# One decoder layer on one core: second attention and experts joined into one program, the last batch routed inside the expert loop

## The chip, the core and the metric

The kernel runs on one core of a Trainium2 chip. The core has five engines with an instruction queue each: TensorE (PE, matmuls and transposes), VectorE (DVE), ScalarE (ACT), GpSimd (POOL), and SyncE (SP), which here only issues DMAs. An engine works through its queue in order, and a wait on a semaphore holds everything behind it on that queue. TensorE's clock is granted at one of two levels, 1.2 and 2.4 GHz; the profile gives it as a share of full speed. The metric is the device time of one execution in microseconds.

## The reference, cut to what matters

Eight batches of 512 tokens with 256 features pass through a pre-norm decoder layer with three parts, each added to its input:

```python
x = x + attn(layernorm(x))            # first attention, linear in the tokens
x = x + xattn(layernorm(x), ctx)      # second attention: 16 heads of 64, causal, keys and values from ctx
x = x + ffn(layernorm(x))             # 16 experts, 4 per token
# ffn, for hidden states h:
probs = softmax(h @ router_w + router_b)
topw, topi = top_k(probs, 4); topw = topw / topw.sum()
out = sum over experts e of (gelu(h @ w1[e] + b1[e]) @ w2[e] + b2[e]) * combine[:, e]
```

w1 is 16 x 256 x 512, w2 is 16 x 512 x 256, all in float32.

## The kernel before

Matmuls on float32 data are done in three passes: each operand is split into a high part (a copy rounded by ScalarE or VectorE to fp32r) and a low part (the difference, by VectorE or GpSimd), and `split3` multiplies low by high, high by low and high by high. So each weight costs splitting work before it can be used.

There are three programs in a row, each in a block of its own: `first_attention`, `cross_attention` and `experts`. At the end of a block all engines meet at a barrier.

**Second attention.** `attention_plan` writes out by hand the order of the steps, and every engine walks through the same list and does its part of each step. Work goes by pairs of heads: n = 0 to 63, eight pairs (p = 0 to 7) for each of eight batches. For a pair there are `scores`, `soften` (maximum and exp), `even` (division by the sum), `turn` (transposes of the probabilities), `weigh` (the product with v) and `keep` (the split of the result). Between them stand the steps of neighbours: projections, `output` of the batch before, its normalisation (`find3`, `norm3`), and its routing: `transpose_x3`, `route`, `choose`, `mark`, `weigh_gates`, `place`, `turn_gates`, `add_b2`. `scatter` steps send a batch's rows, each with its token number and gate weights, by GpSimd's indirect DMA into a table in DRAM (`expert_rows`), sorted by expert; there are 16 such DMAs for a batch.

After pair 63 only the last batch's tail is left: `output`, `find3`, `norm3` and the whole routing chain. The w2 weights of the 16 experts are loaded over the attention's weights by seven DMAs in pairs 4 to 7, and are split (`high_w2` on ScalarE, `low_w2` on VectorE) after pair 63. `tables` computes for the first 20 expert tiles which expert and which rows they have; these tiles are certain from the first seven batches. `first_loads` loads x and w1 of tiles 0 and 1.

**Experts.** A tile is 256 rows of one expert; there are 79 tiles. The loop of `experts` in round j does, for different tiles: `load_w1` j+4, `load_x` j+4 (both issued by SP), `transpose` j+1 (TensorE turns x; ScalarE makes the high part, VectorE copies token number and gates to `tail` and makes the low part), `hidden` j (24 matmuls with 256 columns, gelu and high part on ScalarE, low part on VectorE), `split_w1` j+2 (VectorE), `results` j-1 (24 matmuls, scaling by the gate on ScalarE, two indirect adding DMAs by GpSimd into `out`). The loads have NX = 5 buffers for x and NW = 3 for w1, so load_x(j) waits for the transpose of tile j-5 and load_w1(j) for the split of tile j-3. Three of the five x buffers are free only later: one belongs to `experts`, two lie in `xn3`, the last batch's rows, and so the loads of tiles 3 and 4 wait for the 16 scatters of the last batch, which stand first in GpSimd's queue.

Inside the loop the tables of the other tiles are computed (rounds 5 to 12), and `pad` stores two experts' padding rows a round (four DMAs by SP, rounds 6 to 13). From tile 20 on a load waits for these. The additions of a tile wait for those of the two tiles before it where these may touch the same tokens. Behind the last filled tile there are some empty ones, which always wait.

Of the kernel before, what the change touches and what calls it, by code (L numbers as in the profile page):

```python
# [30 lines left out]
FULL_AT_LEAST = -(-((B - 1) * S * TOPK - E * (ROWS - 1)) // ROWS)  # L31
SURE_TILES = 20
# [7 lines left out]
NY = 3  # L40
# [80 lines left out]
class Kept:  # L121


    def __init__(self, nc, stack, ahead):
        sb = lambda name, shape, dtype=F32: stack.enter_context(nc.sbuf_tensor(f"kept_{name}", shape, dtype))
        self.xn3 = sb("xn3", [P, N_TILES, PAY])
        self.rows_i = [sb(f"rows{i}", [P, N_TILES, TOPK], I32) for i in range(2)]
        self.x_in = [sb(f"x{i}", [P, RT, PAY]) for i in range(2)]
        self.used, self.warm = sb("used", [P, E]), sb("warm", [P, 1])
        self.b1T = ahead.bits[:].rearrange("p a b -> p (a b)").bitcast(F32)[:, 0:E * FC]  # L130
# [106 lines left out]
def f32(ap):  # L237
    return ap.bitcast(F32)
# [738 lines left out]
def cross_attention(nc, sems, spent, d, x1_dram, x1_stored, out, rows_dram, routing, W, projecting, ahead, kept, hold):  # L977

    with ExitStack() as stack:
        p = Phase(nc, stack, sems, "xa")  # L980
        sb, signal, landed = p.sb, p.counts, p.landed
        plan = attention_plan()
# [11 lines left out]
        norms = {n: tuple(sb(f"ln{n}_{part}", shape) for part, shape in  # L994
                          (("stats", [P, N_TILES, 6]), ("mv", [P, N_TILES, 2]), ("rstd", [P, N_TILES]))) for n in (2, 3)}
# [4 lines left out]
        sums = [sb(f"sums{i}", [P, N_TILES, 2]) for i in range(2)]  # L1000
        xn3 = kept.xn3
# [10 lines left out]

        heads = ExitStack()
        own = lambda name, shape, dtype=F32: heads.enter_context(nc.sbuf_tensor(f"xa_{name}", shape, dtype))
        v = [own(f"v{i}", [P, N_TILES, INNER // 2]) for i in range(2)]
        q = [[own(f"q{i}{part}", [P, S], F32R) for part in ("hi", "lo")] for i in range(2)]
        k = [[own(f"k{i}{part}", [P, S], F32R) for part in ("hi", "lo")] for i in range(2)]
# [42 lines left out]
        w2_in, w2_hi = [landed(f"w2_in{i}", [i]) for i in range(len(LOAD_W2))], signal("w2_hi", W2_ORDER)  # L1060
# [5 lines left out]
        first_in = landed("first_x0", [0]), landed("first_x1", [1]), landed("first_w0", [0]), landed("first_w1", [1])  # L1066
# [7 lines left out]
        freed_by = []  # L1074
        for step, at in plan:
# [4 lines left out]
            if by is not None:  # L1080
                bank_of[step, at] = turn
                freed_by.append(by)
                turn += 1

        def bank(step, at):
            return work[bank_of[step, at] % len(work)]

        def sync(sp):
            w = Waits(sp)
            for step, at in plan:  # L1090
                if step == "load":
                    b = at
                    w.wait_ge(x2_ev, (b - 2, 1, 1), b >= 2)
                    w.wait_ge(x1_stored[b % 2], b)
                    sp.dma_start(x1[b % 2][:], x1_dram[b]).then_inc(x1_in[b % 2].of(b), 16)
                    w.wait_ge(c_lo, b - 1, b >= 2)
                    sp.dma_start(ctx32[:], d['ctxT'][b].rearrange("(k p) s -> p k s", p=P)).then_inc(ctx_in.of(b), 16)
                elif step == "add_b2" and at[1] == 1:
                    b = at[0]
                    w.wait_ge(b2_ev, at)  # L1100
                    sp.dma_start(out[b * S:(b + 1) * S, :].rearrange("(t p) c -> p t c", p=P), x2[:]
                                 ).then_inc(x2_out.of(b), 16)
                elif step == "load_w2":
                    end, (first, last) = B * PAIRS - 1, LOAD_W2[at]
                    w.wait_ge(k_pe, end - PAIRS)
                    w.wait_ge(v_pe, v_tiles[-1])
                    w.wait_ge(k_pe, end, at >= 2)
                    w.wait_ge(s_pe, (end - 1, 1, 1), at >= 3)
                    w.wait_ge(q_pe, end, at >= 4)
                    w.wait_ge(s_pe, (end, (3, 2, 1)[at - 4], 1) if at >= 4 else None, at >= 4)  # L1110
                    sp.dma_start(f32(W2_lo[:, first * WE:last * WE]).rearrange("p (k n) -> p k n", n=D),
                                 d['w2'][first:last].rearrange("e (k p) n -> p (e k) n", p=P)).then_inc(w2_in[at].of(at), 16)
                elif step == "first_loads":
                    w.wait_ge(pos_pe, B - 2)
                    sp.dma_start(kept.b1T, d['b1T']).then_inc(b1_in.of(0), 16)
                    w.wait_ge(t_dve, ("landed", 2))
                    w.wait_ge(c_lo, B - 1)
                    w.wait_ge(x2_ev, (B - 2, 1, 1))
                    w.wait_ge(scattered[of_batch(B - 2)], (B - 2, *last_scatter))
                    for j, tile in enumerate((ahead.ctx32[:], ahead.x1_0[:].rearrange("p t c -> p (t c)").rearrange("p (k n) -> p k n", k=KC))):  # L1120
                        row = sp.value_load(routing["first_row"][0:1, j:j + 1], min_val=0, max_val=E * REGION - ROWS)
                        sp.dma_start(kept.x_in[j][:], rows_dram[bass.ds(row, ROWS), :].rearrange("(p a) c -> p a c", p=P)
                                     ).then_inc(first_in[j].of(j), 16)
                        own = sp.value_load(routing["owner"][0:1, j:j + 1], min_val=0, max_val=E - 1)
                        sp.dma_start(tile, d['w1'][bass.ds(own, 1)].rearrange("a (k p) n -> p (a k) n", p=P)
                                     ).then_inc(first_in[2 + j].of(j), 16)
            w.wait_ge(b1_in, 0)
            for i, load in enumerate(first_in):
                w.wait_ge(load, i % 2)

        def tensor(pe):
            w = Waits(pe)

            def work_bank(step, at):
                n = bank_of[step, at]
# [4 lines left out]
            for step, at in plan:  # L1140
                if step == "transpose_x":
                    b, c = at
                    w.wait_ge(ln[2]["norm"], b)
                    PJ = work_bank(step, at)
                    for t in range(N_TILES):
                        m = pe.transpose(PJ[:, t * P:(t + 1) * P], xn[:, t, c * P:(c + 1) * P], ident[:])
                    m.then_inc(x_pe.of(at), 1)
                elif step in ("project_k", "project_q"):
                    n = at
                    b, pr = divmod(n, PAIRS)  # L1150
                    if step == "project_k":
                        w.wait_ge(c_hi, b, b >= 1)
                        w.wait_ge(c_lo, b, b >= 1)
                        src, weights, projected = cT[b % 2], W["WkT"], k_pe
                    else:
                        w.wait_ge(x_hi, (b, KC - 1), b >= 1)
                        w.wait_ge(x_lo, (b, KC - 1), b >= 1)
# [765 lines left out]
```

## Time and profile before

| what | us |
|---|---|
| median of 3 runs | 1717.81 |
| lowest, highest | 1715.85, 1723.5 |
| the profiled execution, own time | 1717.56 |
| its span, first to last instruction | 1715.8 |
| TensorE busy | 1605.2 (94%) |
| VectorE, ScalarE, GpSimd busy | 1193.0, 1066.7, 507.0 |
| second attention, from about | 224 |
| border between second attention and experts | 1142 to 1226 |
| mean granted clock over the whole | 0.974 |

All times are counted from the span's first instruction. A row of a timeline gives start, length, engine, line, operation, written tile <- read tiles, and in brackets the idle time before it with what ended it. SPq, PEq and POOLq are the queues' own work: issuing DMAs, waiting. Busy times of TensorE contain what a lower clock adds.

### The profile page before, as it was taken

The numbers are of one execution on the slowest core, as the hardware profiler recorded it, in microseconds if no ns is written. First come the engines' busy times: TensorE is split into PE (matmuls) and PEld (weight loads), VectorE is DVE, ScalarE is ACT, GpSimd is POOL, SyncE is SP. The second block draws the span as 40 slices with busy tenths as digits, with TensorE's granted clock in tenths as the row PEclk, the third lists the DMA queues.
The fourth block names the chain that finished last, engine by engine and source line by source line (L and its number), as shares of the span: only waits on it lengthen the run. The fifth ranks groups of instructions, "written<-read, shape, count | busy, mean of one in ns | idle before, by whom it ended". The sixth has DMA issues, their size and how long they took to land. (4 is left out here: it accounts for less than half of the span.)

```text
span 1715.8 us, 35765 instructions
## 1 busy us (share of the span) xinstructions
PE 1605.2 (94%) x12470; PEld 1351.0 (79%) x12470; DVE 1193.0 (70%) x2754; ACT 1066.7 (62%) x2699; POOL 507.0 (30%) x430
## 2 busy tenths in 40 slices
PE   5899989999999999999999999985899999999995
PEld 4788866777777777776777777764899999999995
DVE  6888857667767677677766776677576666666662
ACT  4545547666766666666666666763566666666663
POOL 2434400000310301202103003033654546454544
PEclk9999989999999999999999999996999999999998
DMA  3121110000110100201101001063697777777773
GB/s 98 37 87 68 44 61 2 1 25 2 49 42 2 65 26 13 78 2 44 47 2 65 27 2 66 14 226 120 191 256 189 173 167 168 180 174 167 178 174 38
DMA packets 94976, 144.54 MB, mean 84 GB/s; under 512 B 12576, under 2 KB 55120, under 8 KB 94800
## 3 DMA queue, kind: packets, MB, share of 16 engines
q1 hardware_dynamic: 64176, 101.40, 18.6%
q0 software_dynamic: 28896, 38.62, 12.1%
q8 instruction: 103, 1.69, 0.4%
q10 hardware_dynamic: 1728, 2.23, 0.4%
q14 instruction: 73, 0.60, 0.1%
HBM read 90.76 MB, written 51.46 MB: 83 GB/s over the span
## 5 line engine op out<-in xcount | busy, mean ns | idle before, releaser
L1323 ACT ACTIVATE xa_prob<-xa_S,xa_nmax 128x512 f32<-128x512 f32 (+3 forms) x512 | 265.8, 534 | 127.2 <-DVE xa_nmax L1437 126.3
L1849 POOL DMA_INDIRECT out<-ex_y,ahead_bits x158 | 256.8, 1625 | 237.4 <-ACT ex_y L1778 117.7
L1730 PE MATMUL ex_H<-ex_xT,ex_w 128*128 128x256 f32 x1896 | 249.5, 288 | 2.1 <-DVE ex_xT L1815 2.1
L1744 PE MATMUL ex_Y<-experts_w_hi,ex_hT 128*128 x1264 | 239.5, 283 | 0.0
L1730 PEld LDWEIGHTS ex_H<-ex_xT,ex_w 128*128 128x128 f32 x1896 | 235.4, 194 | 2.7 <-issue 2.7
L1744 PEld LDWEIGHTS ex_Y<-experts_w_hi,ex_hT 128*128 128x128 f32 x1264 | 201.9, 191 | 0.0
L1437 DVE TENSOR_REDUCE xa_nmax<-xa_S 128x2 f32<-128x1024 f32 (+3 forms) x256 | 197.9, 815 | 1.2 <-PE xa_S L1196 1.2
L1600 POOL DMA_INDIRECT expert_rows<-kept_xn,kept_rows x112 | 110.8, 989 | 269.0 <-DVE xa_prob L1449 244.7
L1337 ACT ACTIVATE xa_probT<-xa_work 128x512 f32<-128x512 f32 x256 | 139.4, 601 | 79.1 <-PE xa_work L1208 79.1
L1821 DVE TENSOR_TENSOR ex_hT<-ex_h,ex_hT 128x512 fp32r<-128x512 f32 x158 | 109.0, 692 | 109.7 <-ACT ex_hT L1769 109.5
L1744 PE MATMUL ex_Y<-experts_w_lo,ex_hT 128*128 x632 | 178.4, 282 | 0.0
L1449 DVE TENSOR_SCALAR xa_prob<-xa_prob,xa_sums 128x512 f32<-128x512 f32 (+3 forms) x512 | 169.5, 385 | 6.8
L1778 ACT ACTIVATE ex_y<-ex_Y,ahead_bits 128x256 f32<-128x256 f32 x158 | 66.3, 471 | 160.9 <-PE ex_Y L1744 144.3
L1208 PE MATMUL xa_work<-ahead_ident,xa_prob 128*128 128x128 f32 x1280 | 158.9, 278 | 6.3 <-DVE xa_prob L1449 6.2
L1220 PE MATMUL xa_work<-xa_probT,xa_v 128*64 128x512 f32 (+3 forms) x1024 | 153.7, 443 | 0.7 <-ACT xa_probT L1334 0.7
L1208 PEld LDWEIGHTS xa_work<-ahead_ident,xa_prob 128*128 128x128 f32 x1280 | 139.8, 142 | 16.6 <-DVE xa_prob L1449 9.1
L1764 ACT ACTIVATE ex_h<-ex_H,ex_b 128x256 f32<-128x256 f32 x316 | 131.6, 470 | 9.5 <-PE ex_H L1730 8.7
L1444 DVE RECIPROCAL xa_sums<-xa_sums 128x2 f32<-128x2 f32 (+1 forms) x192 | 32.2, 168 | 144.4 <-ACT xa_prob L1323 144.4
L1220 PEld LDWEIGHTS xa_work<-xa_probT,xa_v 128*64 128x64 f32 x1024 | 68.4, 137 | 80.9 <-issue 67.1
L1744 PEld LDWEIGHTS ex_Y<-experts_w_lo,ex_hT 128*128 128x128 f32 x632 | 120.5, 191 | 0.0
L1323 ACT ACTIVATION_READ_ACCUMULATOR xa_prob<-xa_S,xa_nmax 128x1 f32 x512 | 108.4, 212 | 0.0
L1769 ACT ACTIVATE ex_hT<-ex_h 128x512 fp32r<-128x512 f32 x158 | 99.9, 633 | 5.1
(348 smaller groups left out, 3628.7 us busy)
## 6 DMA issues: line engine op xcount, KB each, us to landing
ahead_ctx<-in_w SPq DMA_DIRECT2D x27, 512.0 KB, 3.7
ahead_x<-in_w SPq DMA_DIRECT2D x26, 512.0 KB, 4.4
ahead_xn<-in_w SPq DMA_DIRECT2D x26, 512.0 KB, 4.0
kept_x<-expert_rows SPq DMA_DIRECT2D x32, 273.0 KB, 4.5
kept_xn<-expert_rows SPq DMA_DIRECT2D x31, 273.0 KB, 4.4
experts_w_lo<-in_w SPq DMA_DIRECT2D x5, 1024.0 KB, 6.0
ex_x<-expert_rows SPq DMA_DIRECT2D x16, 273.0 KB, 4.5
expert_rows<-ahead_spare SPq DMA_DIRECT2D x32, 136.5 KB
```

Source lines behind the costliest of these rows:

```text
L1208: m = pe.transpose(PJ[:, col:col + P], prob[n % 2][:, odd, PROB_AT[i] + j * P:PROB_AT[i] + (j + 1) * P], ident[:])
L1220: m = pe.matmul(OB[HD * odd:HD * odd + HD, j * P:512], v[n % 2][:, j, first_col + HD * odd:first_col + HD * odd + HD], probT[:, odd, PROB_ ...
L1323: m = act.activation(prob[n % 2][:, odd, PROB_AT[i]:PROB_AT[i] + width], SB[slot[at]][:, odd, col:col + width], ACT.Exp, bias=nmax[n % 2][ ...
L1337: act.activation(probT[:, odd, first_col:first_col + 512], bank(step, at)[:], ACT.Copy).then_inc(t_ev.of(at), 1)
L1437: m = dve.tensor_reduce(nmax[n % 2][:, i, :], SB[slot[at]][:, :, SCORE_COL[i]:SCORE_COL[i] + (i + 1) * P], AX.X, ALU.max, negate=True)
L1449: m = dve.tensor_scalar(part, part, sums[n % 2][:, i, odd:odd + 1], None, ALU.mult)
L1600: pool.indirect_dma_start(rows_dram, bass.IndirectOffsetOnAxis(rows_i[b % 2][:, t, k:k + 1], 0), xn3[:, t, :], None).then_inc(scattered[of ...
L1730: m = pe.matmul(bank[:, (f % 2) * ROWS:(f % 2 + 1) * ROWS], ww[:, c, f * P:(f + 1) * P], xx[:, c, :], start=(i == 0), stop=(i == len(terms ...
L1744: m = pe.matmul(bank[:, a * D:(a + 1) * D], hh[:, f, a * P:(a + 1) * P], W2[:, bass.ds(own * WE + f * D, D)], start=(i == 0), stop=(i == l ...
L1764: i = act.activation(h32[:, f, :], HB[2 * (j % 2) + u][:, (f % 2) * ROWS:(f % 2 + 1) * ROWS], ACT.Gelu, bias=b1[j % 2][:, f:f + 1])
L1821: dve.tensor_tensor(hT[j % 2][1][:, fs, :], h32[:, fs, :], f32(hT[j % 2][0][:, fs, :]), op=ALU.subtract).then_inc(h_lo.of((j, u)), 1)
L1849: pool.indirect_dma_start(out, bass.IndirectOffsetOnAxis(tail[j % NT][:, a, 0:1].bitcast(I32), 0), y[j % NY][:, a, :], None, compute_op=AL ...
```

## The change

- Second attention and experts become one block with one list of steps. The barrier between them goes; each expert step waits for the attention's semaphores that it needs (`gone`).
- The routing of the last batch (`CHAIN`) moves into rounds 1 to 10 of the expert loop, one piece a round, with a PSUM bank of its own (`ALONE`), and its 16 scatters into rounds 8 to 15, two a round. The expert tiles that come before must be certain without it: `tables` now runs after six batches and covers 24 tiles (`SURE_TILES`).
- w2 is loaded in another order and split in pieces: two pieces in pair 5, two in pair 6, three in pair 7, two beside the turns of pair 63, and seven around the last output projection. Two of the low parts (10 and 13) are made by GpSimd.
- The buffers that the two programs can't share any more are fewer: NX 5 to 2, NW 3 to 2. `load_x` is issued for tile j+2 in round j, `load_w1` for tile j+4 stands behind `split_w1` j+2. Tiles 0 to 11 are turned in one PSUM bank in place of two.
- The late tables move to rounds 8 to 14, the pads to rounds 9 to 16. The gelu table is loaded before round 0, and once more after the exp of the last batch's routing.
- The descriptor buffer of GpSimd's DMAs is set to 8192 bytes.

The diff, cut to its core (indentation that only follows from the new functions is left out):

```diff
-SURE_TILES = 20
+SURE_BATCHES = B - 2
+SURE_TILES = 24
...
-LOAD_W2 = ((2, 5), (5, 8), (12, 14), (14, 16), (8, 10), (10, 12), (0, 2))
+LOAD_W2 = ((2, 4), (4, 8), (14, 16), (0, 2), (12, 14), (8, 10), (10, 12))
-W2_ORDER, LOW_W2 = (3, 4, 5, 6, 7, 14, 15, 0, 1, 2, 8, 9, 10, 11, 12, 13), 13
+TURN_AT, LOW_BY_POOL = 14, (10, 13)
+CHAIN = {1: [("find3", B - 1)], 2: [("norm3", B - 1)], 3: [("transpose_x3", (B - 1, c)) for c in range(KC)], 4: [("route", B - 1)],
+         5: [("choose", B - 1)], 6: [("mark", B - 1), ("weigh_gates", B - 1)], 7: [("place", B - 1)], 8: [("turn_gates", B - 1)],
+         9: [("add_b2", (B - 1, 0))], 10: [("add_b2", (B - 1, 1))]}
...
         if n == B * PAIRS:
-            plan += [*turns, ("tables", None), *high_w2(0, 4), finish[0], *low_w2(0, 3), finish[1], *scatters]
+            plan += [*turns, *split_w2(6, 7), *finish, *scatters]
...
-            second += {4: [("load_w2", 0)], 5: [("load_w2", 1)], 6: [("load_w2", i) for i in (2, 3)],
-                       7: [("load_w2", i) for i in (4, 5, 6)]}.get(p, [])
+            second += {0: [("tables", 0)], 1: [("tables", 1)], 2: [("tables", 2), ("load_w2", 0)], 3: [("tables_turn", None)],
+                       5: [*split_w2(2, 3), ("load_w2", 1), *((step, j) for j in range(2) for step in ("load_x", "load_w1"))],
+                       6: [*split_w2(4, 5), *(("load_w2", i) for i in (2, 3))], 7: [*(("load_w2", i) for i in (4, 5, 6)), ("load_b1", None), *split_w2(14, 15)]}.get(p, [])
...
+             ("split_w1", 0), ("turn_x", 0), ("warm", None), *split_w2(8, 0), ("output", (b, 1, 0)),
+             ("output", (b, 1, 1)), ("load_w1", 2), ("split_w1", 1), *split_w2(10, 9, 13, 12, 11), ("load_w1", 3)]
+    for j in range(MOE_TILES + 1):
+        chain = CHAIN.get(j, [])
+        steps = [("load_x", j + 2), ("turn_x", j + 1), ("turn_tables", None), ("hidden", j), *chain[:1], ("split_w1", j + 2),
+                 ("load_w1", j + 4), ("results", j - 1), *chain[1:]]
...
+        plan += [("scatter_last", i) for i in (2 * (j - 8), 2 * (j - 8) + 1) if 0 <= i < ALL_ROWS]
+        plan += [("pad", e_) for e_ in (2 * (j - 9), 2 * (j - 9) + 1) if 0 <= e_ < E]
...
-NX, NW, NT, FIRST, TURN_AT = 5, 3, 5, 2, 12
+NX, NW = 2, 2
...
-            step_of = {"load_w1": j + 4, "load_x": j + 4, "transpose": j + 1, "hidden": j, "split_w1": j + 2, "results": j - 1}
...
                 elif step == "load_w1":
+                w.wait_ge(gone["t_dve"], ("landed", 2))
+                w.wait_ge(gone["c_lo"], B - 1)
+                w.wait_ge(gone["x2_ev"], (B - 2, 1, 1))
                     w.wait_ge(t_dve, ("landed", 2), j >= SURE_TILES)
                     w.wait_ge(w1_hi, j - NW, j >= NW)
...
                     bank = YB[j % 2]
                     w.wait_ge(y_ev, j - 2, j >= 2)
-                    w.wait_ge(low_w2, W2_ORDER[-1])
+                w.wait_ge(gone["low_w2"], 11)
+                w.wait_ge(gone["low_w2_pool"], 13)
...
-    nc = bacc.Bacc("TRN2", target_bir_lowering=False, num_devices=1)
+    nc = bacc.Bacc("TRN2", target_bir_lowering=False, num_devices=1, dynamic_dma_scratch_size=8192)
```

The new main loop, the same for every engine:

```python
plan = [*attention_plan(), ("finish", None)]
for step, at in plan:
    attend["sync"](sp, w, step, at)
    apply_experts["sync"](sp, w, step, at)
```

## Rows read from the trace of the kernel before

**Rows 1.** The page, part 1: busy time, share of the span, instructions.

```profile
PE 1605.2 (94%) x12470; PEld 1351.0 (79%) x12470; DVE 1193.0 (70%) x2754; ACT 1066.7 (62%) x2699; POOL 507.0 (30%) x430
```

**Rows 2.** Windows: stretch, length, busy us (instructions) by engine, clock, DMA share, GB/s.

```profile
1142.00:1226.00 84.00, 53.55 (x340) 46.72 (x341) 56.69 (x138) 40.70 (x71) 42.16 (x40) 0.74 0.49 157
...
1400.00:1690.00 290.00, 288.81 (x2431) 288.60 (x2430) 189.59 (x325) 190.03 (x420) 151.18 (x95) 1.00 0.72 167
```

**Rows 3.** The chain that ended last, 1183 to 1240: start, length, what.

```profile
1213.46 2.65 DMA expert_rows<-kept_xn,kept_rows
...
1216.85 3.19 DMA kept_xn<-expert_rows
...
1226.47 0.44 PE ex_X L1716 x4
...
1226.91 2.87 PE ex_H L1730 x24
...
1232.65 0.44 PE ex_X L1716 x4
```

**Rows 4.** Timeline of PE around the border: start, length, work [idle before].

```profile
1150.40 2.37 PE L1220 MATMUL xa_work<-xa_probT,xa_v 128*64 128x512 f32 x16 [0.74 <-ACT xa_probT L1334]
...
1155.65 0.36 PE L1237 MATMUL xa_work<-xa_Wo_hi,xa_oT_lo 128*128 128x256 f32 x1 [2.44 <-DVE xa_oT_lo L1464]
...
1191.24 1.09 PE L1716 MATMUL ex_X<-ahead_ident,kept_x 128*128 128x128 f32 x4 [8.31 <-PEq L1605]
```

**Rows 5.** Timeline of ACT and of DVE between 1154 and 1166.

```profile
1154.59 7.69 ACT L1367 ACTIVATE experts_w_hi<-experts_w_lo 128x1024 fp32r<-128x1024 f32 x8
...
1156.01 3.49 DVE L1534 TENSOR_TENSOR experts_w_lo<-experts_w_lo,experts_w_hi 128x1024 fp32r<-128x1024 f32 x3
...
1163.95 1.41 DVE L1382 BATCH_NORM_STATS2 xa_ln_stats<-xa_x 128x6 f32<-128x256 f32 x4
```

**Rows 6.** Groups of POOL's instructions by form: count, busy us, mean ns.

```profile
L873 POOL TENSOR_TENSOR WqT_lo<-ahead_ctx,WqT_hi 128x1024 fp32r<-128x1024 f32 x2 | 4.8, 2412 | 0.0
```

**Rows 7.** Timeline of all engines over two tiles.

```profile
1303.18 0.60 PE L1716 MATMUL ex_X<-ahead_ident,ex_x 128*128 128x128 f32 x4
...
1305.31 0.84 ACT L1764 ACTIVATE ex_h<-ex_H,ex_b 128x256 f32<-128x256 f32 x2
...
1309.57 1.23 DVE L1804 TENSOR_TENSOR ex_w<-ahead_ctx,ex_w 128x1024 fp32r<-128x1024 f32 x1
...
1311.60 0.39 SPq L1699 DMA_DIRECT2D ahead_ctx<-in_w  x1
...
1312.82 0.34 SPq L1685 DMA_DIRECT2D kept_x<-expert_rows  x1
...
1315.54 0.60 PE L1716 MATMUL ex_X<-ahead_ident,kept_xn 128*128 128x128 f32 x4
```

**Rows 8.** Waits of SP's queue, 1290 to 1660: total us, times, longest.

```profile
SPq L75 <- DVE ex_w L1804: 222.8, 59, 6.1
```

**Rows 9.** DMA issues, three windows of the expert loop: count, KB, median us to landing.

```profile
kept_xn<-expert_rows SPq DMA_DIRECT2D x23, 273.0 KB, 4.5
...
kept_xn<-expert_rows SPq DMA_DIRECT2D x1, 273.0 KB, 3.0
...
kept_xn<-expert_rows SPq DMA_DIRECT2D x1, 273.0 KB, 6.0
```

**Rows 10.** Timeline of SP's queue with the pad stores.

```profile
1243.60 2.79 SPq L1692 DMA_DIRECT2D expert_rows<-ahead_spare  x4
...
1247.21 0.41 SPq L1699 DMA_DIRECT2D ahead_xn<-in_w  x1
```

**Rows 11.** Timeline of PE, the last hidden step.

```profile
1687.69 3.02 PE L1730 MATMUL ex_H<-ex_xT,ex_w 128*128 128x256 f32 x24
```

**Rows 12.** The chain that ended last, its end.

```profile
1701.18 3.77 DMA out<-ex_y,ahead_bits
...
1707.68 1.55 POOL out L1849
```

More of the change, by code:

```diff
@@ L1059, in cross_attention @@
         id_set = signal("id_set", batches)
[L1060 removed]
+        w2_in, w2_hi = [landed(f"w2_in{i}", [i]) for i in range(len(LOAD_W2))], signal("w2_hi", [at for step, at in plan if step == "high_w2"])
+        low_w2, low_w2_pool = (signal(n, [at for step, at in plan if step == "low_w2" and (at in LOW_BY_POOL) == mine])
+                               for n, mine in (("low_w2", False), ("low_w2_pool", True)))
         x3_pe, x3_ev = signal("x3_pe", blocks), signal("x3_ev", blocks)
@@ L1079, in cross_attention @@
                   "tables_turn": (t_dve, ("landed", 2))}.get(step)
-            if by is not None:
+            if (step, at) in ALONE:
+                alone_after[step, at], last_alone = last_alone, by
+            elif by is not None:
                 bank_of[step, at] = turn
@@ L1085, in bank @@
         def bank(step, at):
+            if (step, at) in alone_after:
+                return SB[0][:, 1, :]
             return work[bank_of[step, at] % len(work)]
[L1088 to L1129, printed above, removed]
@@ L1138, in work_bank @@
                 return work[n % len(work)]
[L1140 to L1157, printed above, removed]
-                        src, weights, projected = xT, W["WqT"], q_pe
-                    PJ = work_bank(step, at)
-                    for c in range(KC):
-                        for i, (ww, xx) in enumerate(split3(weights, src)):
-                            m = pe.matmul(PJ[:], ww[:, c, pr * P:(pr + 1) * P], xx[:, c, :],
-                                          start=(c == 0 and i == 0), stop=(c == KC - 1 and i == 2))
-                    m.then_inc(projected.of(n), 1)
-                elif step == "project_v":
-                    n, t = at
-                    b, half = divmod(n, 2)
@@ new lines, in tensor @@
+            if step == "transpose_x":
+                b, c = at
+                w.wait_ge(ln[2]["norm"], b)
+                PJ = work_bank(step, at)
+                for t in range(N_TILES):
+                    m = pe.transpose(PJ[:, t * P:(t + 1) * P], xn[:, t, c * P:(c + 1) * P], ident[:])
+                m.then_inc(x_pe.of(at), 1)
+            elif step in ("project_k", "project_q"):
+                n = at
+                b, pr = divmod(n, PAIRS)
+                if step == "project_k":
@@ L1605, in cross_attention @@
-        with nc.Block() as block:
-            block.tensor(tensor)
-            block.scalar(scalar)
-            block.vector(vector)
-            block.gpsimd(gpsimd)
-            block.sync(sync)
-        return x2_out, scattered
-NX, NW, NT, FIRST, TURN_AT = 5, 3, 5, 2, 12
-def experts(nc, sems, d, rows_dram, out, routing, held, ahead, kept, x2_out, sent):
+            elif step == "tables_turn":
+                w.wait_ge(tables_pe, 0)
+                tables.give_out(dve, t_dve, 0, bank(step, at), ahead, routing)
@@ L1619, in experts @@
+NX, NW = 2, 2
+CHAIN_END = 12
+LATE_ROOM = 2584
+def experts(nc, sems, d, rows_dram, out, routing, held, ahead, kept, gone):
     with ExitStack() as stack:
@@ L1657, in experts @@
         w1_hi, w1_lo, b1_ev = (signal(n, tiles) for n in ("w1_hi", "w1_lo", "b1_ev"))
-        w1_loaded = [landed(f"w1_loaded{i}", [j for j in tiles[i::NW] if j >= FIRST]) for i in range(NW)]
+        w1_loaded = [landed(f"w1_loaded{i}", tiles[i::NW]) for i in range(NW)]
         h_pe, gelu, h_hi, h_lo = (signal(n, halves) for n in ("h_pe", "gelu", "h_hi", "h_lo"))
         y_pe, y_ev = signal("y_pe", tiles), signal("y_ev", tiles)
-        plan = [("load_x", 2), ("load_w1", 2), ("split_w1", 0), ("transpose", 0), ("split_w1", 1), ("load_w1", 3), ("load_x", 3)]
```

1349 lines of the change are left out of this document (717 added, 632 removed).

## Prediction

> **What bounds the kernel now.** I read the page first. TensorE is busy for 1605.2 of 1715.8 us [rows 1], so time can come only from its idle stretches or from a slower clock. The windows place them: 84 us around the border between attention and experts hold 53.55 us of TensorE work at a mean granted clock of 0.74, while 290 us of the expert loop are 288.81 us busy at 1.00 [rows 2]. The chain around the border shows the loop's rhythm. The steps called X start at 1226.47 and 1232.65, so a tile takes 6.18 us, all of it matmuls (0.44 + 2.87 + 2.87), and the first tiles before that hang on the last scatters and on the loads behind them [rows 3]. TensorE's timeline gives the border's two ends: the last weighing of values starts at 1150.40, the output projection at 1155.65, the first expert transpose only at 1191.24 [rows 4].
>
> Names: t(j) is the time at which TensorE starts turn_x(j+1), the first step of round j. Before, t(4) = 1226.47 (rounds 0 to 3 turn tiles 1 to 4; x of tile 4 was the load that landed at 1220.04, and X of tile 5 starts at 1226.47).
>
> **Removed at the border.** The barrier, the routing of the last batch in an empty TensorE, and 16 scatters that stand ahead of tiles 3 and 4. TensorE's work there is not removed. The clock comes back with it.
>
> **The border after.** Rows 4 fix the start: output projection from 1155.65, since it waits for the last low part of the attention output, and VectorE reaches that as early as before. W2's splitting costs ScalarE 0.98 us a piece (7.69/8) and VectorE 1.16 us (3.49/3) [rows 5]. Seven pieces move into pairs 5 to 7 of the last batch, where TensorE sets the pace: taken as free there (if the cover is gone, 7 x 1.16 = 8 us). Two pieces go to GpSimd at 2.41 us each [rows 6], behind the 16 scatters that end near 1164; they are done near 1169, before round 1's results ask for them. The two projections are 48 matmuls like those of a tile half (2.87 us per 24), so t(0) = 1155.65 + 5.8 = 1161.5. VectorE then has, behind the attention output (ready 1155.1): 0.7 for b2, 2.1 for splitting w1 of tile 0, 0.9 for x, two pieces 2.3, two output additions that end near 1162.5, and w1 of tile 1, ready at 1164.6.
>
> **The part that decides: NX 5 to 2 and NW 3 to 2.** I followed one tile through all queues. From X at 1303.18, ScalarE's gelu starts at 1305.31, VectorE ends the low half of w1 at 1309.57 + 1.23 = 1310.8, SP issues the next w1 load at 1311.60 and the next x load 1.22 later, at 1312.82. TensorE is at the next-but-one X at 1315.54 [rows 7]. That is w1 issue = t(j) + 8.4, x issue = t(j) + 9.6. Before, these loads are for tiles far ahead. SP waits on this same split 59 times in 360 us [rows 8], and nobody is hurt.
>
> After, load_w1(j+4) waits for the split of w1(j+2), which VectorE makes in round j. load_x(j+3) stands behind it in SP's queue, although its own buffer has long been free. And x(j+3) is what TensorE needs first in round j+2. So
>
> t(j+2) = t(j) + 9.6 + landing of x.
>
> The landing is 4.5 us in the median of 23 loads; the shortest that I found took 3.0, one of the longest 6.0 [rows 9]. At 6.18 us a round only 12.36 - 9.6 = 2.7 us are to be had. None of the landings is so short. The period becomes (9.6 + 4.5)/2 = 7.05 us, 0.87 more, and TensorE is idle for 0.87 us in each round. At 6.18 of 7.05 us busy I leave the clock at 1.00. The splitting can't come earlier: it stands behind the tile's hidden step on VectorE, which follows matmul, gelu and copy.
>
> A page speaks to this term. The Trainium skill (DMA: Bandwidth & Descriptors, Anatomy of one DMA) fits one software-queued transfer as 2.0 us plus its bytes over 436 GB/s. For 273 KB that would be an estimate of 2.6 us, which lands in time, and the sum would be that of the first rival below. The trace disagrees: 4.5 us with the w1 load just ahead on the same queue, and 3.19 us with no load just ahead [rows 3].
>
> **First rounds.** x(2) is behind load_w1(3), which waits for 1164.6: t(1) = 1164.6 + 0.9 + 1.2 + 4.5 = 1171.2. VectorE has three more W2 pieces (3.5 us) before x(1), and ends w1(2) at 1172.1: t(2) = 1172.1 + 6.6 = 1178.7. Statistics for the last batch (batch norm 1.41 us [rows 5], about 2.0 with what follows) stand ahead of w1(3): t(3) = 1171.2 + 14.1 + 2.1 = 1187.4. Normalising (1.4) lies partly in slack: t(4) = 1194.3. That is 32.2 us earlier than 1226.47.
>
> **Rounds 4 to 78.** 75 rounds x 0.87 = +65.3 us. Routing steps ahead of a split in rounds 4 to 9 (0.7 to 2.2 us each: logits, exp with two table loads on ScalarE, marking, placing), each counting half, less what the even and odd chains absorb: +1.7. Tables in rounds 8 to 14: +2. The 32 pad stores: SP issues four in 2.79 us, and the next load starts 3.6 us after the first pad [rows 10]. After, they stand between load_w1(j+4) and load_x(j+3) in rounds 9 to 16, so x is issued 3.8 us later and lands behind their bytes, I take 0.5 more: 4.3/2 x 8 = +17. Before, rounds 4 to 78 held 3.4 us beyond 75 x 6.18, mostly waits for tables and for late additions, which a slower loop hides: -3.4. Sum: +82.6.
>
> The 16 scatters now fill GpSimd in rounds 8 to 15, two each, in the time that its additions leave. A smaller descriptor buffer for GpSimd's DMAs: at most two additions are issued per tile, so I take nothing; were each of 158 additions late by 0.3 us, they would still be within a round.
>
> **The end.** The last hidden step starts at 1687.69 [rows 11]; with it and two result steps TensorE ends at 1696.3, 19.5 us before the span's end. The last seven tiles wait for each other's additions, 6.6 us a link (4 us from issue to landing, and the last issue ends at 1709.2) [rows 12]. With 7.05 us a round GpSimd keeps up, and the end is 1.7 (scaling) + 1.8 (waiting for tile 77) + 3.4 (two issues) + 6.6 (as before) = 13.5 us behind TensorE: -6.
>
> **Sum.** 1715.8 - 32.2 + 82.6 - 6 = 1760.2 us of span. The profiled execution's own time was 1717.56, 1.8 above its span, and is within 0.3 us of the median of the runs (1717.81). So 1762 us. A measurement of this kernel can tell about 0.5% (8.6 us) from no change.
>
> **Rivals.**
> 1. The x loads land in time and the loop stays at 6.18 us: it would need landings below 2.7 us. Then VectorE's splits alone hold the first rounds: t(1) = 1169.0, when x(1)'s low part is ready, and three rounds of some 6.6 us follow, so t(4) is near 1189, 37.5 us earlier, the end is as before, and the time is 1680. For it: before, both loads travel among GpSimd's additions, and a slower loop could thin that traffic. Against: even the shortest landing is 3.0. Chance 0.12.
> 2. The landings shorten to 3.0 to 3.6 us. At 3.3 the period is 6.46: -35 at the border, 75 x 0.28 = +21, pads and the rest +14, so no change, 1718; at 3.0 it is 1705, at 3.6 about 1730. Chance 0.08, half of it within 0.5%.
> 3. Idle TensorE loses its clock. It did so at the border (0.74 [rows 2]). In the eight pad rounds of 9.2 us it is idle for 3. At half the clock there the first half of hidden is 1.4 us longer and results more: +10 to +30, so 1772 to 1795. Chance 0.15.
> 4. TensorE is slowed in pairs 5 to 7 by the moved splits by up to 8 us, with the rest as forecast: 1770. It is in the forecast's range.
>
> **Chances.** The forecast (landings of 3.6 to 5 us, 1730 to 1785) has 0.65. Landings of 5.0 us would give 7.3 us a round and 1784; that bounds it above. The range takes in rivals 2 and 4 and most of 3: 1703 to 1790, with 0.12 left out below and some 0.06 above. Faster by over 0.5%: 0.12 + 0.03 = 0.15. Within 0.5%: 0.05. Slower: 0.80.
>
> **What would show it.** Right: in rounds 20 to 70 X starts every 7.0 to 7.1 us; TensorE's idle time there, 60 us in all, is ended by the DMA of expert rows; SP's x load goes out 1.2 us behind the w1 load; t(4) near 1194 and no gap of more than 5 us at the border; rounds 9 to 16 the slowest. Wrong: X every 6.18 us in spite of landings over 2.7 us (then the order of SP's queue is not what binds), or a border that still has tens of idle microseconds, or a low clock in the loop.

## The result and the profile after

The changed kernel takes 1799.93 us in the median of four runs (1795.01 to 1804.69); the kernel before takes 1716.96 us beside it. The ratio is 1.0475, 95% interval 1.0436 to 1.0514. The forecast was 1762 with a range of 1703 to 1790. The sign and the mechanism held; the loss is 83 us where 45 were forecast, and the range ends below it. The profiled execution has a span of 1793.3 us where the sum gave 1760.2, so 33 us are to be found. It is the fastest of the four; the other 5 us to the median are in no trace and stay unexplained.

The page of the changed kernel, lines of its parts 1, 5 and 6 (the ones that answer to [rows 1] and [rows 9]):

```profile
PE 1623.1 (91%) x12470; PEld 1360.6 (76%) x12470; DVE 1195.2 (67%) x2752; ACT 1078.5 (60%) x2702; POOL 505.0 (28%) x432
...
L1732 PE MATMUL ex_X<-ahead_ident,kept_x 128*128 128x128 f32 x316 | 53.1, 293 | 89.4 <-DMA kept_x<-expert_rows 81.1
...
kept_x<-expert_rows SPq DMA_DIRECT2D x79, 273.0 KB, 4.5
```

TensorE has the same 12470 matmuls and is idle for 170 us, before for 111. Of the 170 us, 81.1 are ended by one thing, the landing of an x load in front of the turn of x (the steps called X). Its median landing is the 4.5 us of before [rows 9].

Windows of the changed kernel: the border, rounds up to 4, rounds 4 to 10, the pad rounds 10 to 18, rounds 18 to 77, and one single round in the last line (columns as in [rows 2]):

```profile
1140.00:1166.00 26.00, 20.00 (x140) 14.64 (x141) 20.39 (x34) 21.47 (x41) 15.97 (x15) 0.87 0.61 197
1166.00:1204.40 38.40, 27.22 (x195) 26.64 (x194) 28.94 (x48) 17.88 (x36) 15.97 (x9) 0.82 0.42 119
1204.40:1250.60 46.20, 40.46 (x351) 39.80 (x350) 29.71 (x87) 28.93 (x60) 20.70 (x18) 1.00 0.60 140
1250.60:1333.10 82.50, 60.85 (x424) 59.94 (x423) 37.40 (x81) 34.02 (x72) 40.76 (x31) 0.83 0.73 192
1333.10:1762.40 429.30, 378.52 (x3070) 370.29 (x3069) 242.34 (x414) 248.10 (x531) 186.43 (x118) 0.98 0.63 147
1356.10:1363.80 7.70, 7.70 (x53) 7.70 (x53) 2.64 (x5) 3.54 (x7) 3.09 (x2) 0.78 0.63 139
```

Before, the loop was busy 288.81 of 290 us [rows 2]. Now 59 rounds (t(18) to t(77)) take 429.3 us, 7.28 each, with TensorE busy for 378.52. The pad rounds take 82.5/8 = 10.3 us.

What one waits for, in rounds 18 to 77 (line waited for, us in total, times, longest), TensorE's and then SP's own:

```profile
PE ex_X L1732 <- DMA kept_x<-expert_rows: 50.6, 37, 2.2
...
SPq L76 <- DVE ex_w L1821: 287.3, 58, 7.7
```

SP stands on the split of w1 once a round, as before [rows 8], where it hurt nobody. Two rounds on the timeline (start, length), to lay beside [rows 7]:

```profile
1371.83 0.65 PE L1732 MATMUL ex_X<-ahead_ident,kept_x 128*128 128x128 f32 x4 [1.74 <-DMA kept_x<-expert_rows]
...
1378.03 0.60 PE L1732 MATMUL ex_X<-ahead_ident,kept_x 128*128 128x128 f32 x4
1378.28 1.23 DVE L1821 TENSOR_TENSOR ex_w<-ahead_x,ex_w 128x1024 fp32r<-128x1024 f32 x1
...
1380.29 0.38 SPq L1714 DMA_DIRECT2D ahead_x<-in_w  x1
1381.50 0.33 SPq L1697 DMA_DIRECT2D kept_x<-expert_rows  x1
...
1386.05 0.66 PE L1732 MATMUL ex_X<-ahead_ident,kept_x 128*128 128x128 f32 x4 [1.72 <-DMA kept_x<-expert_rows]
```

The split ends at 1379.51, the w1 load goes out at 1380.29 (t + 8.46), the x load 1.21 us behind it, and the next-but-one X starts 4.55 us after that. The two chains, of even and of odd tiles, are not evenly spaced: in many stretches rounds of 6.20 and of about 8.2 us take turns, and what counts is the sum of two (median 14.43 us in rounds 18 to 77).

### The profile page after: what moved, and what is told of

It reads as the page before. It is cut to its first block, busy times and chain, and to the rows that moved or that the text cites. A ratio compares the mean times of both kernels' runs of the same rounds, so it can differ in the third digit from the quotient of the medians.

```text
span 1793.3 us, 35763 instructions
## 1 busy us (share of the span) xinstructions
PE 1623.1 (91%) x12470; PEld 1360.6 (76%) x12470; DVE 1195.2 (67%) x2752; ACT 1078.5 (60%) x2702; POOL 505.0 (28%) x432
## 3 DMA queue, kind: packets, MB, share of 16 engines
q0 software_dynamic: 28896, 38.62, 11.4%
## 4 chain that ended last, share of the span: by engine, by line
PE 38%; ACT 18%; DVE 13%; DMA 10%; issue 5%; SPq 3%; POOL 0%; POOLq 0%; DVEq 0%; ACTq 0%
DMA kept_x<-expert_rows 9%; PE ex_H L1750 7%; ACT xa_prob L1334 7%; PE xa_work L1174 5%; PE xa_work L1249 5%; PE xa_S L1203 4%; PE xa_work L1185 4%; PE xa_work L1232 4%; PE xa_work L1220 4%; ACT xa_probT L1348 3%; DVE xa_nmax L1452 3%; DVE ex_w L1821 2%; ACT ex_h L1785 2%; PE ex_X L1732 2%; DVE xa_prob L1464 2%
## 5 line engine op out<-in xcount | busy, mean ns | idle before, releaser
L1867 POOL DMA_INDIRECT out<-ex_y,ahead_bits x158 | 249.6, 1580 | 327.4 <-ACT ex_y L1798 193.2
L1750 PE MATMUL ex_H<-ex_xT,ex_w 128*128 128x256 f32 x1896 | 265.8, 300 | 0.0
L1750 PEld LDWEIGHTS ex_H<-ex_xT,ex_w 128*128 128x128 f32 x1896 | 251.7, 207 | 0.0
L1785 ACT ACTIVATE ex_h<-ex_H,kept_b 128x256 f32<-128x256 f32 x316 | 131.7, 468 | 58.5 <-PE ex_H L1750 50.8
L1732 PE MATMUL ex_X<-ahead_ident,kept_x 128*128 128x128 f32 x316 | 53.1, 293 | 89.4 <-DMA kept_x<-expert_rows 81.1
L1732 PEld LDWEIGHTS ex_X<-ahead_ident,kept_x 128*128 128x128 f32 x316 | 36.0, 146 | 99.6 <-DMA kept_x<-expert_rows 91.3
```

The source lines that it names most:

```text
L1732: m = pe.transpose(x_bank(j)[:, c * ROWS + a * P:c * ROWS + (a + 1) * P], x_in[j % NX][:, a, c * P:(c + 1) * P], ident[:])
L1750: m = pe.matmul(bank[:, (f % 2) * ROWS:(f % 2 + 1) * ROWS], ww[:, c, f * P:(f + 1) * P], xx[:, c, :], start=(i == 0), stop=(i == len(terms ...
L1785: i = act.activation(h32[:, f, :], HB[2 * (j % 2) + u][:, (f % 2) * ROWS:(f % 2 + 1) * ROWS], ACT.Gelu, bias=b1[j % 2][:, f:f + 1])
L1867: pool.indirect_dma_start(out, bass.IndirectOffsetOnAxis(tail[j % NT][:, a, 0:1].bitcast(I32), 0), y[j % NY][:, a, :], None, compute_op=AL ...
```

## The experiments

Theory A, going into them: x arrives late because its load stands in SP's queue behind a w1 load that waits for VectorE; what counts is the time from its issue to the round that needs it, and a smaller number of buffers matters only through that. Theory B: two buffers for each of x and w1 are themselves too few at this load on the DMA queues, or the rest of the joined program costs the time. All ratios are against the kernel before, run beside it, with 95% intervals.

**1. The x load one tile further ahead.** The step that issued x of tile j+2 ahead of the turn now issues x of tile j+3 behind it, still with two buffers:

```diff
-        steps = [("load_x", j + 2), ("turn_x", j + 1), ("turn_tables", None), ("hidden", j),
+        steps = [("turn_x", j + 1), ("load_x", j + 3), ("turn_tables", None), ("hidden", j),
...
-             ("output", (b, 1, 1)), ("load_w1", 2),
+             ("output", (b, 1, 1)), ("load_x", 2), ("load_w1", 2),
```

> The changed kernel with one order changed: in round j SP issues the x load of tile j+3 right behind the transpose of tile j+1, ahead of the w1 load that waits for VectorE's split. Buffers (two for x, two for w1), traffic and all other work stay. Theory A (the x load is late only because it stands behind that w1 load in SP's queue): X starts every 6.2 us in rounds 20 to 70, TensorE's idle time ended by the DMA of expert rows (81 us) all but goes, the clock stays at 1.00 there, and the time is 1690 us, between 1680 and 1705. Theory B (two x buffers are too few, or the DMA engines are too busy, whatever the order): rounds stay at 7.0 us or more and the time above 1780 us.

Measured: 1694.23 us (1692.85 to 1695.74), 0.9847 [0.9823, 0.9871]. Two windows of this kernel, rounds up to 4 and 347 us of the loop:

```profile
1166.00:1204.40 38.40, 30.34 (x236) 30.17 (x235) 30.96 (x53) 20.79 (x44) 15.79 (x8) 0.87 0.49 142
...
1333.00:1680.00 347.00, 341.13 (x2888) 340.71 (x2886) 222.74 (x381) 226.09 (x498) 181.99 (x113) 1.00 0.72 166
```

Its timeline, SP's loads and TensorE's X:

```profile
1372.97 0.38 SPq L1714 DMA_DIRECT2D ahead_x<-in_w  x1
1374.18 0.33 SPq L1697 DMA_DIRECT2D kept_x<-expert_rows  x1
...
1376.70 0.60 PE L1732 MATMUL ex_X<-ahead_ident,kept_x 128*128 128x128 f32 x4
...
1382.83 0.60 PE L1732 MATMUL ex_X<-ahead_ident,kept_x 128*128 128x128 f32 x4
```

The x load still goes out 1.21 us behind the w1 load, and still takes 4.4 us in the median. But it now carries the tile of X at 1382.83 instead of 1376.70, so it has 8.65 us in place of 2.52. X follows every 6.13 us, TensorE no longer waits for x in the loop, and the clock is 1.00. A move of one step in SP's queue takes off some 106 us, more than the change had lost; theory A holds for this loss.

**2. The two buffers alone, in the kernel before.** NX = NW = 2 and the order of loads of the changed kernel; the barrier and the routing of the last batch stay as before. (One thing follows from the buffers: the x loads of tiles 3 and 4 no longer wait for the last batch's scatters.)

```diff
-NX, NW, NT, FIRST, TURN_AT = 5, 3, 5, 2, 12
+NX, NW, NT, FIRST, TURN_AT = 2, 2, 5, 2, 12
...
-            step_of = {"load_w1": j + 4, "load_x": j + 4, "transpose": j + 1, "hidden": j, "split_w1": j + 2, "results": j - 1}
+            step_of = {"load_x": j + 2, "transpose": j + 1, "hidden": j, "split_w1": j + 2, "load_w1": j + 4, "results": j - 1}
```

> The kernel before with one part of the change alone: NX = 2 and NW = 2 in the expert loop, load_x for tile j+2 at the head of round j, load_w1 for tile j+4 behind split_w1 j+2. Barrier, routing of the last batch, tables and pads stay where they were (the first x loads no longer wait for the last batch's scatters, since their buffers are free). Theory A: rounds of 7.3 us, rounds with pads of 10.3 us, so 67 x 1.1 + 8 x 4.1 = +107 us, less some 8 at the start and 6 at the end: about 1807 us. Theory B (the loss comes from the last batch's routing and scatters inside the loop, or from the joined program): 1717 us or less.

Measured: 1819.31 us (1818.79 to 1826.34), 1.059 [1.0558, 1.0622]. The loop, window of this kernel:

```profile
1420.00:1660.00 240.00, 211.61 (x1691) 207.57 (x1690) 134.47 (x229) 135.35 (x292) 101.58 (x64) 0.96 0.63 144
```

So buffers and order alone, without the joined program, cost 101 us, and by the two ratios (1.059 and 1.0475) the joined program gives some 20 back.

**3. Pads behind the next x load.** In the changed kernel, the four pad stores of a round are issued after the x load that follows them:

```diff
+        pads_of = lambda i: [("pad", e_) for e_ in (2 * (i - 9), 2 * (i - 9) + 1) if 0 <= e_ < E]
+        steps[1:1] = pads_of(j - 1)
...
-        plan += [("pad", e_) for e_ in (2 * (j - 9), 2 * (j - 9) + 1) if 0 <= e_ < E]
```

> The changed kernel with the pad stores of a round moved behind the next x load in SP's queue, so that they fill the time in which SP waits for the split. Theory A: rounds 9 to 16 fall from 10.3 us to some 7.5, in all -22 us, so 1778 us. If the pads cost by their traffic on the DMA engines and not by their place in the queue, the rounds stay near 10 us and the time near 1800.

Measured: 1783.29 us (1781.04 to 1785.29), 1.0366 [1.034, 1.0393]. Rounds 10 to 18 fall from 10.3 to 7.70 us, 21 us in all; the mean granted clock there is 0.97 in place of 0.83, so a part of the 21 is clock. t(10) is 3.3 us later than in the changed kernel, and rounds 18 to 77 came out at 7.39 instead of 7.28, which takes some back.

**4. Both late low parts by VectorE.** GpSimd splits none of w2:

```diff
-TURN_AT, LOW_BY_POOL = 14, (10, 13)
+TURN_AT, LOW_BY_POOL = 14, ()
```

> The changed kernel with the low parts of w2 pieces 10 and 13 made by VectorE in place of GpSimd. If GpSimd's additions hold VectorE up (three pieces took 5.6 us there and a 4-column copy 2.3 us while GpSimd worked on its two), five pieces take 5.8 us, and X of round 1 starts some 2 us earlier than 1177.5, in spite of more work. If VectorE is merely busy, X of round 1 starts 2.3 us later. In the time of the whole (1800 us) either is hardly to be seen.

One run: 1798.59 us, which can't be told from the changed kernel; the border's trace can. First the changed kernel's timeline at the border, with the last weighing of values (which began at 1150.40 before [rows 4]):

```profile
1156.10 2.38 PE L1232 MATMUL xa_work<-xa_probT,xa_v 128*64 128x512 f32 x16 [0.79 <-ACT xa_probT L1345]
...
1162.73 0.17 DVE L1826 COPY kept_b<-ahead_bits 128x4 f32 x1 [0.22 <-issue]
...
1166.02 0.60 PE L1732 MATMUL ex_X<-ahead_ident,kept_x 128*128 128x128 f32 x4
...
1168.49 5.98 POOL L1604 TENSOR_TENSOR experts_w_lo<-experts_w_lo,experts_w_hi 128x1024 fp32r<-128x1024 f32 x2
1168.82 2.33 DVE L1826 COPY kept_b<-ahead_bits 128x4 f32 x1
1171.06 5.62 DVE L1549 TENSOR_TENSOR experts_w_lo<-experts_w_lo,experts_w_hi 128x1024 fp32r<-128x1024 f32 x3
...
1176.70 0.68 DVE L1832 TENSOR_TENSOR ex_xT<-ex_X,ex_xT 128x512 fp32r<-128x512 f32 x1
...
1177.52 1.09 PE L1732 MATMUL ex_X<-ahead_ident,kept_x 128*128 128x128 f32 x4 [8.03 <-DVE ex_xT L1832]
```

And the same place with GpSimd out of it:

```profile
1164.03 0.60 PE L1732 MATMUL ex_X<-ahead_ident,kept_x 128*128 128x128 f32 x4
1166.83 0.17 DVE L1825 COPY kept_b<-ahead_bits 128x4 f32 x1
1166.90 5.76 DVE L1549 TENSOR_TENSOR experts_w_lo<-experts_w_lo,experts_w_hi 128x1024 fp32r<-128x1024 f32 x5
1173.49 1.08 PE L1732 MATMUL ex_X<-ahead_ident,kept_x 128*128 128x128 f32 x4 [6.00 <-DVE ex_xT L1831]
```

VectorE does all five pieces in 5.76 us, 1.15 each, where three took 5.62 beside GpSimd; a copy of 4 columns takes 0.17 in place of 2.33. From t(0) to t(1) it is 9.46 us in place of 11.50.

**5. Three orders together.** Experiments 1 and 4, and the pads between the x and the w1 load of the next round:

```diff
+        steps[2:2] = pads_of(j - 1)
```

> The changed kernel with three edits together: the x load ahead of the w1 load (1694 us alone), all low parts of w2 by VectorE (2.1 us at the border), and the pad stores of a round between the x load and the w1 load, where SP waits for the split anyway. With the x load first, rounds 13 to 16 still take 9.3, 7.6, 8.9 and 7.7 us, 8.9 us too much. If these are the w1 loads, late behind the pads in SP's queue, they go: 1694 - 2 - 8 = 1684 us. If they come from the pads' traffic on the DMA engines (busy to 1.00 there), they stay: 1692.

Measured: 1690.45 us (1687.09 to 1692.27), 0.9842 [0.9821, 0.9863]. The pad rounds fall to 6.5 us (7.3 in experiment 1) and t(1) to 1173.1 (1176.3). In the two traces that puts experiment 5 ahead by 8.5 us at t(77). The ratios to the kernel before, 0.9847 for experiment 1 and 0.9842 here, each with an interval of some 4 us to either side, don't show it: what pads and GpSimd's share are worth once x has 8.65 us of room stays between nothing and a few microseconds.

**6. x ahead of the w1 load, but behind the same wait.** Here the x load gets no more tiles of lead. It is issued at the moment when the w1 load may go, and in front of it:

```diff
-        steps = [("load_x", j + 2), ("turn_x", j + 1), ("turn_tables", None), ("hidden", j), *chain[:1], ("split_w1", j + 2),
-                 ("load_w1", j + 4), ("results", j - 1), *chain[1:]]
+        steps = [("turn_x", j + 1), ("turn_tables", None), ("hidden", j), *chain[:1], ("split_w1", j + 2),
+                 ("load_x", j + 3), ("load_w1", j + 4), ("results", j - 1), *chain[1:]]
...
+                w.wait_ge(w1_lo, j - 1, j >= 3)
```

> The changed kernel with the x load still behind the wait for the split of w1(j+2), but issued before the w1 load in place of after it. This tests the sum t(j+2) = t(j) + 8.5 (wait for the split) + 1.2 (issue of the w1 load) + landing. If the landing is long because 512 KB of w1 are ahead of it, it falls to some 3.2 to 3.5 us: 8.5 + 3.4 = 11.9, under two free rounds of 12.36, the rounds are near 6.3 us and the time is 1700 to 1715 us. If the landing keeps its 4.5 us whatever stands ahead, two rounds take 13.0, a round 6.5, and the time is 1740 us. If only the order behind the wait decides and no margin counts, it stays at 1785 or more.

Measured: 1705.47 us (1703.93 to 1707.1), 0.9934 [0.9911, 0.9957]. Page part 6 of this kernel, and its timeline with SP's two loads:

```profile
kept_x<-expert_rows SPq DMA_DIRECT2D x79, 273.0 KB, 2.8
```

```profile
1376.53 0.60 PE L1733 MATMUL ex_X<-ahead_ident,kept_x 128*128 128x128 f32 x4
1376.99 1.23 DVE L1822 TENSOR_TENSOR ex_w<-ahead_x,ex_w 128x1024 fp32r<-128x1024 f32 x1
1379.01 0.33 SPq L1698 DMA_DIRECT2D kept_x<-expert_rows  x1
1380.10 0.38 SPq L1715 DMA_DIRECT2D ahead_x<-in_w  x1
...
1382.66 0.60 PE L1733 MATMUL ex_X<-ahead_ident,kept_x 128*128 128x128 f32 x4
```

The X before these starts at 1370.4; the x load leaves 8.6 us behind it and is for the X at 1382.66. It lands in 2.8 us with the w1 load behind it, where it took 4.5 with that load ahead. 8.6 + 2.8 = 11.4 is less than two rounds of 6.13, and X follows every 6.14 us. The w1 load takes 5.0 in place of 3.7, which it can afford. This is the forecast's formula at its edge: 9.7 + 4.5 binds, 8.6 + 2.8 does not, with the same two buffers and the same wait. The kernel is still 11 us slower than that of experiment 1. In the traces the difference of span, 8.4 us, is spread over all stages: 1.5 us at t(4), 3.8 up to t(18), and 3.3 in rounds 18 to 77, where one round took 9.32.

**7. Two buffers in the kernel before, with x one tile further ahead.** Experiment 2 with the order of experiment 1:

```diff
-            step_of = {"load_x": j + 2, "transpose": j + 1, "hidden": j, "split_w1": j + 2, "load_w1": j + 4, "results": j - 1}
+            step_of = {"transpose": j + 1, "load_x": j + 3, "hidden": j, "split_w1": j + 2, "load_w1": j + 4, "results": j - 1}
```

> The kernel before with NX = 2 and NW = 2 (1819 us when the x load stood behind the w1 load) and the x load of tile j+3 right behind the transpose of tile j+1. Theory A: two buffers of each are enough when the order is right, the rounds are 6.2 us again, and the first tiles no longer wait for the 16 scatters: 1705 to 1717 us. If two buffers cost by themselves: above 1740 us.

Measured over ten runs: 1714.34 us (1708.06 to 1719.61), 0.998 [0.9965, 0.9996]. Its loop:

```profile
1420.00:1660.00 240.00, 240.00 (x2030) 240.00 (x2029) 159.77 (x274) 159.52 (x353) 127.70 (x80) 1.00 0.75 176
```

When each load is issued for the right tile, two buffers in place of five and three cost nothing in these 240 us and nothing in the whole, and theory B falls as the cause of the loss. The whole is a balance, though. In this trace t(4) is 9.4 us earlier than before, since tiles 3 and 4 no longer wait for the scatters; rounds 4 to 10 give back 3.7 of this, rounds 18 to 77 4.7 (two neighbouring rounds took 7.76 and 12.19 us in this execution), and the end 0.9. Whether the small losses belong to the buffers is open. Beside it, experiment 5 shows what the joined program, its pads moved too, is worth with the loads in order: 1714.34 - 1690.45 = 23.9 us.

**8. The seven moved splits of w2 put back.** Experiment 5 with w2's pieces 2 to 5, 14, 15 and 1 split behind pair 63 (pairs 6, 7 and 63 are cut in the same way as pair 5 here):

```diff
-                       5: [*split_w2(2, 3), ("load_w2", 1), *((step, j) for j in range(2) for step in ("load_x", "load_w1"))],
+                       5: [("load_w2", 1), *((step, j) for j in range(2) for step in ("load_x", "load_w1"))],
...
-             ("split_w1", 0), ("turn_x", 0), ("warm", None), *split_w2(8, 0), ("output", (b, 1, 0)),
+             ("split_w1", 0), ("turn_x", 0), ("warm", None), *split_w2(2, 3, 4, 5, 14, 15, 1, 8, 0), ("output", (b, 1, 0)),
```

> As the one with three edits, but the seven w2 pieces of pairs 5 to 7 are split behind pair 63 again. Prices the moved splits. In the changed kernel the last weighing ends 5.7 us later than before. If the moved splits are the reason, it ends some 4 to 6 us earlier here, but VectorE has 7 x 1.16 = 8.1 us more ahead of the first tiles, so the whole is 2 to 4 us slower than with three edits: 1687 us. If the pairs are late for another reason, the weighing stays where it is and the whole is 8 us slower.

Measured: 1691.95 us (1689.83 to 1694.89), 0.9849 [0.9828, 0.987], 1.5 us above experiment 5 and not to be told from it by the intervals; 2 to 4 us were expected. The traces show two amounts of opposite sign. TensorE's weighings of the last three pairs, first in experiment 5, then in 8:

```profile
1130.60 2.38 PE L1233 MATMUL xa_work<-xa_probT,xa_v 128*64 128x512 f32 x16
1144.83 4.54 PE L1233 MATMUL xa_work<-xa_probT,xa_v 128*64 128x512 f32 x16
1153.56 2.37 PE L1233 MATMUL xa_work<-xa_probT,xa_v 128*64 128x512 f32 x16 [0.78 <-ACT xa_probT L1346]
```

```profile
1132.33 2.37 PE L1233 MATMUL xa_work<-xa_probT,xa_v 128*64 128x512 f32 x16
1144.01 2.37 PE L1233 MATMUL xa_work<-xa_probT,xa_v 128*64 128x512 f32 x16
1150.94 2.37 PE L1233 MATMUL xa_work<-xa_probT,xa_v 128*64 128x512 f32 x16 [0.90 <-ACT xa_probT L1346]
...
1178.26 1.09 PE L1733 MATMUL ex_X<-ahead_ident,kept_x 128*128 128x128 f32 x4 [13.95 <-DVE ex_xT L1832]
```

From the first to the third of them it is 22.96 us with the moved splits and 18.61 without: 4.35 us lost in the pairs, 2.2 of them in the middle weighing, which ran at half the clock (4.54 against 2.37). Without the move, t(0) to t(1) is 17.4 us in place of 9.7, 7.7 more. The net is 3.4 us for the move.

## Why the prediction went wrong in size

**Right: what binds.** x(j+3) behind the w1 load, the w1 load behind VectorE's split, needed two rounds on. The terms came out nearly as written: w1 issue at t + 8.46 (forecast 8.4), x 1.21 to 1.23 later (1.22), landing 4.5 in the median (4.5). TensorE's idle time in rounds 18 to 77 is (429.3 - 378.52)/59 = 0.86 us a round (0.87). Rival 1, landing in time at 1680, did not happen here, but experiment 6 shows how near it was. The Trainium skill (DMA: Bandwidth & Descriptors, Anatomy of one DMA) has a fit for a software-queued transfer that gives 2.6 us as an estimate for 273 KB. These loads are issued by SP and take 2.8 us with nothing just ahead in experiment 6 and 4.5 behind the 512 KB load, so the figure comes near the first place in the queue and not the second.

**The step that failed: "The period becomes (9.6 + 4.5)/2 = 7.05".** The formula is right; what failed is the size of its terms, which were put in as if no round were ever slower than the median. In the trace of the changed kernel the mean over 57 of these loads is 9.84 us from X to the x issue and 4.74 from there to the next-but-one X, and (9.84 + 4.74)/2 = 7.29, as measured; the medians are 9.67 and 4.71. The landing was no longer than forecast (mean 4.43, median 4.5). What comes on top of it, 0.31 us in the mean, is TensorE still busy when x has landed.

Most of this comes from five rounds. In them a part of the matmuls ran at half the clock, and they took 7.70 us without a gap (clock 0.78 in the last row of the windows). The next X then came 1.6 to 2.8 us after its x had landed, and the split, and SP behind it, came 1.5 us later (11.2 in place of 9.67). By these figures I estimate 7.13 us a round without the five, so they make about two thirds of the excess. I had written "At 6.18 of 7.05 us busy I leave the clock at 1.00"; it was 0.98 over these rounds. The measured 7.28 in place of 7.05 cost 0.226 x 59 = 13.3 us.

Of the signs that I had named, the x load 1.2 us behind the w1 load and TensorE's idle time ended by the DMA of expert rows came as said. The slowest rounds were 10 to 17 and not 9 to 16: the pads of round j delay the x that is needed at t(j+2), and so lengthen round j + 1; round 9 took 6.43 us. X every 7.0 to 7.1 us, t(4) near 1194 and no gap over 5 us at the border (one of 8.03) did not come. A low clock in the loop, which I had named as a sign of being wrong, came in those five rounds.

The other terms that were too small, in order of time:

- **"Taken as free": the moved splits.** The last weighing starts at 1156.10 in place of 1150.40 [rows 4]. The two weighings ahead of it, in the kernel before and in the changed kernel:

```profile
1131.25 2.37 PE L1220 MATMUL xa_work<-xa_probT,xa_v 128*64 128x512 f32 x16
1142.89 4.07 PE L1220 MATMUL xa_work<-xa_probT,xa_v 128*64 128x512 f32 x16
```

```profile
1133.12 2.38 PE L1232 MATMUL xa_work<-xa_probT,xa_v 128*64 128x512 f32 x16
1147.37 4.54 PE L1232 MATMUL xa_work<-xa_probT,xa_v 128*64 128x512 f32 x16
```

  So of the 5.7 us, 1.9 are there two pairs earlier, where nothing shows them to be the splits' (over the changed kernel and experiments 1, 4, 5, 6 and 8 this weighing starts between 1130.6 and 1133.1), and 3.8 arise in the last pairs; experiment 8 has 4.35 for the seven moved pieces. The middle weighing lost clock in the kernel before too (4.07), so its slow clock is not the moved splits' alone. The cover over them was thinner than taken, as rival 4 had it (up to 8). t(0) is 1166.0 in place of 1161.5.
- **GpSimd's two pieces, taken to lie beside VectorE.** They and VectorE's three pieces and copies fill 8.2 us (1168.49 to 1176.7) where side by side they were to take about 5; alone they would be 2 x 2.41 + 3 x 1.16 [rows 5, 6], 8.3 in a row. By these sums nothing was gained by running them side by side, and t(1) was 2.0 us nearer to t(0) with all five on VectorE (experiment 4). The clock at the border was 0.82, where I had "the clock comes back with it". In all, t(4) is 10.1 us later than forecast: 4.5 at t(0), 1.8, 1.9, 0.3 and 1.6 in the rounds after it.
- **Pad rounds: 10.3 us in place of 9.2.** This is rival 3 where it was put: the clock is 0.83 there, and 8 rounds cost 82.5 - 75.4 = 7.1 us more than forecast (8 x 7.05, 17 for the pads, 2 for the tables). By experiment 3 the place of the pads in the queue costs 21 us, clock included; the term was 17 without clock.
- **Rounds 4 to 10** took 46.2 us, 2.2 more than forecast, and **the end**, t(77) to the last instruction, 30.9, which is 0.9 more than the forecast's own 30.0 (34.3 before, less 6, and 1.7 for two longer rounds).

Sum: 10.1 + 2.2 + 7.1 + 13.3 + 0.9 = 33.6 for the 33.1 us of span that were missing (the 0.5 lies in how the forecast's small terms are divided over these stretches). All have one sign. I read them as delays on a chain that had no slack left, counted as if each instruction kept its median time and TensorE its clock; no run gives back the clock alone. The range was cut at "landings of 5.0 us" and 1790, and rival 3 was priced for the pad rounds alone; the clock then added to the main loop too. Two small slips of the working change little: the window of the 59 waits [rows 8] is 370 us long, not 360, and the 1172.1 at which VectorE was to end w1(2) is 1 us more than its own terms give (1164.6 + 3.5 + 0.9 + 2.1 = 1171.1).

**What stays open.** Why rounds 18 to 77 are 0.1 us longer in experiment 3 than in the changed kernel is not settled. What makes TensorE's clock fall in some rounds of the loop and not in others is not either. The smaller descriptor buffer for GpSimd's DMAs was not tried by itself.

## What to carry to other kernels

When buffers are cut, write down for each load the round in which it is issued, what stands ahead of it in the issuing queue, and the round that needs it; if the loop is then set by that chain, its period is a sum of means, not of medians, and stalls can cost clock on top. Before giving back memory for more buffers, try the order: here the same two buffers lost 101 us with one order of SP's steps, and with another the time was that of the kernel before (ratio 0.998). Joining the two programs was worth 24 us, and it only showed once the order was mended; that version (experiment 5) beats both kernels, 1.6% below the kernel before.

## What the runs showed of the chip

- **A load's place in SP's queue sets its landing.** 273 KB take 2.8 us ahead of a 512 KB load and 4.5 behind one issued 1.2 us earlier; the 512 KB load goes from 3.7 to 5.0 when the order is turned.
- **VectorE and GpSimd held each other up.** A copy of 128x4 took 2.33 us in place of 0.17 while GpSimd subtracted 128x1024, and their work filled the time of both in a row. The Trainium skill (SBUF — State Buffer, SBUF: two separate sides) says that one pair of ports is shared by the two, and that a GpSimd instruction and a VectorE instruction with two SBUF inputs take it in turns, each for its whole length. The trace agrees: 8.2 us for the subtractions of both, against 8.3 in a row.
- **In five of 59 rounds of the stalling loop the clock fell.** Each of the five came right behind a wait of TensorE for x of 2.0 to 2.2 us, but other waits as long (2.02 us in front of 1662.70) were not followed by it. The changed kernel's timeline shows one such round:

```profile
1356.10 0.66 PE L1732 MATMUL ex_X<-ahead_ident,kept_x 128*128 128x128 f32 x4 [2.23 <-DMA kept_x<-expert_rows]
1356.52 4.62 PE L1750 MATMUL ex_H<-ex_xT,ex_w 128*128 128x256 f32 x24
```

  Its hidden step took 4.62 us, where it takes 3.12 in the round from 1371.83. The round to 1363.80 is busy throughout, at a mean granted clock of 0.78; with the stalls gone (experiment 1) the same loop is at 1.00.
